# Where the rotation's products are made, and a new order of four engines' work, in a two-layer transformer block

## The reference

```python
x = x + ffn(cond(x, side, lens))
# cond: attention of 16 heads of 16; the keys are x and the query's own key of side, masked by length
score = concat([q @ k_prev.T * SCALE masked, (q * k_self).sum(-1) * SCALE]); attn = softmax(score) ...
# ffn: DEPTH = 2 layers, each on all 4096 rows seen as w windows of 128
h = shift_token(x); q, k, v = split(h @ wqkv, 3)          # 8 heads of 64
q, k = l2norm(q) * qs, l2norm(k) * ksc
q = q * cos * scale + rotate_half(q) * sin * scale        # the rotation
k = k * cos / scale + rotate_half(k) * sin / scale
o = local_attention(q, k, v)                              # own and previous window
x = x + o @ wo
h = layernorm(shift_token(x)); a, g = split(h @ w1 + b1, 2)
x = x + (a * gelu(g)) @ w2 + b2
```

## Time and profile before

| | |
|---|---|
| median of 3 runs | 3763.35 us |
| profiled execution, its own time | 3767.51 us |
| its span | 3765.3 us |
| busy share PE / PE weight load / DVE / ACT / POOL | 96 / 65 / 71 / 60 / 21 % |
| granted TensorE clock, mean | 0.978 |

### The profile page before, as it was taken

The page is one execution under the profiler, slowest core; times in us unless marked ns, Lnnn a source line. Parts: engine busy times, 40 slices in busy tenths (PEclk is TensorE's granted clock), DMA queues, the critical chain, the costliest instruction groups (busy, mean ns, idle before and its releaser), DMA issues.

```text
span 3765.3 us, 58543 instructions
## 1 busy us (share of the span) xinstructions
PE 3602.7 (96%) x20454; PEld 2447.4 (65%) x20454; DVE 2670.4 (71%) x7188; ACT 2242.3 (60%) x5085; POOL 788.4 (21%) x882
## 2 busy tenths in 40 slices
PE   5789999999999999999999999999999999999987
PEld 2456666666666666666666666666666666666655
DVE  2567777777777777777777777777777777777654
ACT  1246566566566666656656656666665665666653
POOL 1122221222222122222122222212222222222110
PEclk7799999999999999999999999999999999999998
DMA  5111110111111011111101111101111110111000
GB/s 144 23 24 23 29 29 20 16 24 29 29 29 29 14 20 26 29 29 29 23 13 24 30 29 29 29 17 19 24 29 29 29 26 13 21 29 24 7 6 9
DMA packets 104608, 99.34 MB, mean 26 GB/s; under 512 B 15276, under 2 KB 103040, under 8 KB 104320
## 3 DMA queue, kind: packets, MB, share of 16 engines
q1 hardware_dynamic: 104320, 95.61, 13.8%
HBM read 35.80 MB, written 8.39 MB: 12 GB/s over the span
## 4 chain that ended last, share of the span: by engine, by line
PE 85%; DVE 7%; issue 3%; ACT 3%; SPq 1%; POOL 0%; DMA 0%; DVEq 0%; ACTq 0%; POOLq 0%
PE ps L994 15%; PE ps L894 12%; PE ps L1007 9%; PE ps L908 6%; PE ps L941 5%; PE ps L961 5%; PE ps L950 4%; PE ps L809 3%; PE ps L970 3%; PE ps L928 3%; PE ps L752 3%; PE ps L762 3%; PE ps L799 3%; PE ps L781 2%; PE ps L834 2%
## 5 line engine op out<-in xcount | busy, mean ns | idle before, releaser
L559 POOL TENSOR_TENSOR inv<-ssq_f,minus_half 128x16 f32<-128x16 f32 x128 | 419.8, 3279 | 1043.9 <-DVE ssq_f L1209 1040.4
L994 PE MATMUL ps<-feed_area,w_s 128*128 128x256 f32 x2560 | 600.7, 382 | 7.3 <-DVE feed_area L1273 6.3
L994 PEld LDWEIGHTS ps<-feed_area,w_s 128*128 128x128 f32 x2560 | 480.5, 191 | 123.2 <-issue 54.1
L657 ACT ACTIVATE attn_area<-attn_area,f_nb,inv 128x128 f32<-128x128 f32 (+1 forms) x1024 | 546.3, 536 | 13.2 <-DVE f_nb L1237 11.6
L1146 DVE TENSOR_REDUCE c_mx<-ps 128x2 f32<-128x512 f32 x512 | 343.2, 687 | 180.5 <-PE ps L781 179.7
L679 ACT ACTIVATE feed_area<-ps,b_s 128x256 f32<-128x256 f32 x320 | 151.0, 473 | 386.3 <-PE ps L994 384.8
L1007 PE MATMUL ps<-feed_area,w_s 128*128 128x256 f32 x1536 | 355.2, 381 | 5.2 <-DVE feed_area L1283 1.5
L610 ACT ACTIVATE cond_area<-ps 128x512 f32<-128x512 f32 x512 | 294.9, 593 | 104.3 <-PE ps L799 103.4
L1233 DVE CUSTOM_DVE_ANT_0 attn_area<-ps,cst 128x128 f32<-128x128 f32 (+1 forms) x1024 | 303.8, 353 | 72.7 <-issue 71.2
L1007 PEld LDWEIGHTS ps<-feed_area,w_s 128*128 128x128 f32 x1536 | 281.7, 190 | 48.9 <-DVE feed_area L1283 14.6
L1283 DVE SCALAR_TENSOR_TENSOR feed_area<-ps,b_s,feed_area 128x256 f32<-128x256 f32 (+1 forms) x384 | 183.8, 479 | 169.0 <-ACT feed_area L679 166.3
(11 more groups left out here) (156 smaller groups left out, 6528.4 us busy)
## 6 DMA issues: line engine op xcount, KB each, us to landing
cond_area<-cond_area SPq DMA_DIRECT2D x384, 128.0 KB, 4.2
x_rows<-in_x SPq DMA_DIRECT2D x32, 256.0 KB, 2.8
f_rows<-in_fside_BxSxS SPq DMA_DIRECT2D x32, 256.0 KB, 3.2
res_rows<-in_x SPq DMA_DIRECT2D x32, 256.0 KB, 2.8
out<-res_rows SPq DMA_DIRECT2D x32, 256.0 KB, 2.1
wqkv_s<-in_L_ffn_wqkv SPq DMA_DIRECT2D x2, 1536.0 KB
w_s<-in_L_ffn_w SPq DMA_DIRECT2D x2, 1364.0 KB
cond_area<-cond_area SPq DMA_DIRECT2D x128, 6.0 KB
```

Of the source, the lines that this page charges most:

```text
L559: nc.gpsimd.tensor_tensor(inv[:, l, t, :], ssq_f[:, l, t, :], minus_half[:, :], ALU.pow).then_inc(SL[l]["inv_norm"], 1)
L657: nc.scalar.activation(soft[:, h % SOFT, lo:hi], soft[:, h % SOFT, lo:hi], ACT.Exp, bias=f_nb[:, l, q, h:h + 1], scale=inv[:, l, q, h:h + ...
L994: last = mm(ps[:, N0 + f % 2, c * N:(c + 1) * N], w1_s[:, l, k, lo:lo + P], hn[:, k, :], start=(k == 0), stop=(k == KD - 1))
```

## The change

Three things change. ACT squares into `ra` instead of `rot[t]`, in a step of its own (`rotate`) and no longer directly behind its second copy; for t = 1 it waits until DVE's sum of t = 0 has read `ra`. POOL makes the two sine products into `rot[t]`, as soon as `qk_s` is there, ahead of the power in its step. DVE keeps the sum of squares, the floor and then the cosine product (into `ra`, over the squares); the final sum of the rotation moves from DVE's step `rotate` to its step `combine`. And all four strings in `ORDER` are new: PE's and DVE's cuts stay, ACT's and POOL's stay in part.

```diff
@@ ORDER
-    PE=((57, 24, 27, 1),
-        "SSARASNASSRRAASRSSAASANRNSSAASNAARARAANAANASANAASANAANSSSSAASAASASAAARSRRANARSRNAASRSASARNASASASRRANA"
+    PE=((57, 24, 27, 1),
+        "NASRARRASRSAASSAARNANASRASSANARASSNAANNSNSAASSANSSSSAAASAASASAAAARAANARASAARRNAARSSAAASRSARAARAASAS"
...
@@ POOL, step rotate
+                    qk4 = qk_s[:, t, :].rearrange("p (s h d) -> p s h d", s=2, h=FH)
+                    pool.wait_ge(SL[l]["qk_copied"], upto(seq, "qk_copied", 2 * t + 2))
+                    for s in range(2):
+                        swapped = qk4[:, s].rearrange("p h (b d) -> p h b d", b=2)[:, :, ::-1, :]
+                        nc.gpsimd.tensor_tensor(
+                            rot[t][:, s * INNER:(s + 1) * INNER].rearrange("p (h b d) -> p h b d", h=FH, b=2),
+                            swapped, sin_t[:, l, t, s].rearrange("p (a b d) -> p a b d", a=1, b=2)
+                            .broadcast_to([P, FH, 2, FDH // 2]), ALU.mult).then_inc(SL[l]["rot_sin"], 1)
@@ ACT
-                    if c == 1:
-                        act.wait_ge(SL[l]["qk_copied"], upto(seq, "qk_copied", 2 * t + 2))
-                        nc.scalar.activation(rot[t], qk_s[:, t, :], ACT.Square).then_inc(SL[l]["squared"], 1)
+                elif name == "rotate":
+                    act.wait_ge(SL[l]["qk_copied"], upto(seq, "qk_copied", 2 * t + 2))
+                    if t == 1:
+
+                        act.wait_ge(SL[l]["rotated"], upto(seq, "rotated", t))
+                    nc.scalar.activation(ra, qk_s[:, t, :], ACT.Square).then_inc(SL[l]["squared"], 1)
@@ DVE, step rotate
-                    dve.wait_ge(SL[l]["qk_copied"], upto(seq, "qk_copied", 2 * t + 2))
-                    if t == 1:
-                        dve.wait_ge(SL[l]["rotated"], upto(seq, "rotated", t))
+                    dve.wait_ge(SL[l]["squared"], upto(seq, "squared", t + 1))
+                    V.tensor_reduce(ssq[:, l, t, :], ra.rearrange("p (h d) -> p h d", d=FDH),
+                                    AX_X, ALU.add).then_inc(SL[l]["sum_squares"], 1)
...
                     V.tensor_tensor(ra.rearrange("p (s h d) -> p s h d", s=2, h=FH), qk4,
                                     cos_t[:, l, t].rearrange("p s (a d) -> p s a d", a=1)
                                     .broadcast_to([P, 2, FH, FDH]), ALU.mult).then_inc(SL[l]["rot_cos"], 1)
-                    dve.wait_ge(SL[l]["squared"], upto(seq, "squared", t + 1))
...
-                    for s in range(2):
...
+                elif name == "combine":
+                    dve.wait_ge(SL[l]["rot_cos"], upto(seq, "rot_cos", t + 1))
                     dve.wait_ge(SL[l]["rot_sin"], upto(seq, "rot_sin", 2 * t + 2))
                     V.tensor_tensor(rot[t], ra, rot[t], ALU.add).then_inc(SL[l]["rotated"], 1)
-                elif name == "combine":
```

30 lines of the change are left out of this document (12 added, 18 removed).

## The result

| | before | after |
|---|---|---|
| median | 3765.51 us (4 runs beside it) | 3938.86 us (4 runs, 3934.53 to 3940.09) |
| ratio | | 1.0456, 95% interval 1.0444 to 1.0469 |
| span of the profiled execution | 3765.3 | 3938.0 |
| a full round, mean of 28 | 111.04 | 116.55 |
| mean granted clock | 0.978 | 0.978 |

The change makes the kernel 4.6% slower: 173 us where 83 were forecast, outside the range. Each of the 29 full rounds is 5.51 us longer, which makes 160 of the 173.

The account below looks back on a forecast made before the run. PE was taken as the bound, 96% busy. Per round 0.29 + 3.29 + 0.80 + 0.48 - 2.0 = 2.86 us, over 29 rounds +83 us, gave 3846 us beside the median of 3763.35; range 3780 to 3915.

Parts of the forecast that it names:

- The sign: Whole kernel: the change was forecast to make it slower, by 83 us; chance of slower 0.83.
- the first two terms: PE, each round: 0.29 us more for crossings to or from part-array steps, and 3.29 us of new waits for banks.
- The edits in themselves: DVE loses 5.6 us a round, POOL gains 10.1, ACT's square moves; none is the bound, each worth nothing by itself.
- The table of bank pairs: PE steps that take a bank soon after an earlier step wait for its copy: 3.29 us a round in all.
- the bank rule: A PE step taking an earlier step's bank waits 0.20 us + copy + 0.05, less PE's work between them.
- two things weighed: POOL products holding DVE (none counted, 1.0 us a round possible) and one more ACT table switch a round (priced 0).
- the hold: POOL's SBUF product slows DVE beside it: four scalings 1.92 us against 1.01 alone; up to 1.26 per sine product, none counted.
- place 3: From the layer's normalisation on, DVE's queue delays the maximum of score 1, then a feed-forward product: 0.80 us a round.
- Rival 2: GpSimd's products hold DVE: 1.0 us of held instructions and 1.1 of lesser queue terms a round, 3907 us; chance 0.18.
- The 0.48: Place 2: four ACT exponentials stand ahead of the prob after turn_max, delaying the prob behind it 0.48 us a round.
- The price of the table switches: ACT, nine switches a round for eight: priced 0 because ACT waits for PE there, at most 37 us.
- The waits of the kernel before: PE's old waits, between 1.0 and 2.74 us a round, taken as 2.0 and subtracted from the new ones.

Follow-up runs that it names:

- e3: Changed kernel with POOL's sine products an eighth as wide, the rest left out: 3885.41 us.
- e7: Changed kernel with POOL's own-key product and low part of the queries cut to an eighth of their columns: 3897.75 us.
- e12: Changed kernel with POOL's sine products, own-key product and low part of the queries all cut to an eighth: 3842.69 us.
- e9: Changed kernel with the square root of layer 1's variance replaced by a plain copy, removing two table loads a round: 3932.22 us.
- e5: Changed kernel with PE's order alone altered at four places to draw bank pairs apart: 3963.63 us.
- e11: Changed kernel without layer 1's square root, and with PE's prob6 moved behind scores01 and qk101 behind prob7: 3933.90 us.
- e13: Changed kernel with ACT's second layer-0 value-row copy ahead of the conditioning value's copy, and PE's prob6 behind scores01: 3906.18 us.
- e14: Kernel before with four steps moved on PE and ACT around the first two probability turns: 3764.43 us against 3764.31.
- e8: Kernel before with two down-projection parts moved later in PE's order, each into a place where PE pauses: 3874.43 us.
- e1: Changed code with the order table of the kernel before, except one moved ACT step: 3912.69 us.
- e2: Code of the kernel before with the new order table: 4094.63 us.

## Why the prediction was wrong

**The sign and the first two terms held.** The edits in themselves came as worked out: POOL's sine products 1280 ns for 1263, DVE relieved of 256 products, no engine a new bound. The table of bank pairs is the best part, measured in the trace after (forecast in brackets): `score` 10 0.32 (0.36), `prob` 2 0.33 (0.39), `prob` 6 0.44 (0.42), second scores 0.18 (0.29), second `qk` 0.63 (0.62), last `turn_max` 0.54 (0.53), `prob` 11 0.44 (0.20), `weigh` 3 0.36 (0.21), and an output projection of each layer 0.24 and 0.19 (0.27 together): 3.66 for 3.29. The pause before layer 1's second projection on X_ffn, whose absence was to refute the bank rule, is there.

**The step that failed** is the first of "two things weighed": "I count none, since most of DVE's instructions then read PSUM, and at most one or two fall on a late place". The row that priced the hold was shown, 1.01 us against 1.92, and was set to 0 in the sum. It was 1.51 us a round for the sine products (e3, 53 us with the partial rounds) and 1.25 for the products of place 3 (e7, 41 us). The error has two parts. POOL's new products were looked at and DVE's three largest instructions on SBUF (L1222, L1226, L1251), which they meet, were not followed through the new order. And POOL's old products, the own-key product and the low part, were not looked at, though the order moves them as well: behind the first rotation's power, which is where DVE now scales keys and tiles. Rival 2 had the mechanism, with 0.18 and 3907 us, and its range, 3880 to 3940, just holds the result; its 1.0 us of held instructions was too small for lack of those two. That the two together took 3.03 us a round (e12) is the size of the term that stood at 0.

**Place 3** was the right place with the wrong reason. 0.80 us were forecast for a long DVE queue. After shows 2.05 (`score` 0 0.86, `score` 2 0.73, `score` 3 0.29, `hidden` 4 0.17), and e12, with the same queue and no hold, 0.10: the queue by itself costs next to nothing. (In e12 the shortened products also hand over their results sooner, but DVE did not wait for them in after either, as its waits above show.)

**The 0.48** for `prob` 10 did not come: PE's pause stands one step on, before `prob` 11, and is in the 0.44 above. The price of the table switches, 0, held: with 2.4 us of loads a round taken away in e9 the round stayed at 116.54.

**The unforecast 1.0** at the end of the round, `turn_probs` 2 (0.44) and in the down projection (0.59), is the hold again: both are 0.01 or less in e3.

**Without the hold the sum stands.** e12 has everything of the change but the hold: 3842.7 us, 78 above the kernel before, and 113.52 us a round, where the forecast had 3846, 83 and 113.9. So the total for the order came out near, and the one effect left at 0 was larger than all the rest together, 96 us against 78. That agreement has some luck in it: 0.48 and 0.80 were forecast and not found, 0.37 more in the pairs while a few waits that had been left out (0.1 to 0.3 each) stand on the other side. The waits of the kernel before, taken off as 2.0, are 2.79 by the comparison of starts.

**What stays open.** Why PE's pauses in e5 and e11 add up to the same is explained for one pair (e13) and only argued for the others. Which of e13's two moves gives its 0.69 us was not run apart. That the removal of a pause before a bank's second use gives back its length was shown in no run by itself. The part up to the end of the third round, which took from 299 to 319 us over the profiles at a mean clock of 0.80 to 0.83, is not explained; between the profiles it differs by up to 20 us, and e14's profile, 11 us short, has rounds of the old length.

## What to carry to other kernels

Before moving an elementwise product to GpSimd, list the VectorE instructions on SBUF that will stand beside it and beside everything of GpSimd's that the new order shifts, and add a full hold for each that somebody waits for; a free engine's work is not free if it stops a bounding queue. When a pause on the bounding engine is to be filled, look first at what the step that fills it hides where it stands, and at whether the copy that is waited for stands behind an instruction that isn't ready: reordering the waiting engine alone moved pauses about or made new ones (e5, e8, e11). Reordering it together with the engine that was waited for removed two pauses once (e13) and gained nothing the other time (e14). Look at the granted clock behind a long pause too: in e1, e2 and e8, with one of 1.9 us or more in each round, about every second round also had 3.4 us at half the clock and was 1.6 to 1.7 us longer.

## What the runs showed of the hardware

- The hold is of whole instructions, as far as the rows of place 3 show, and depends on the form. There L1226 begins 0.99 us before the low part ends (1733.60) and ends 0.54 after it, with 0.69 as its lone length; then L529, begun 0.58 before L1226 ends, ends 1.13 after it, with 1.26 as its lone length. In the trace after, the two-source product of 128x512 on SBUF (L1226) takes 692 ns with no POOL instruction beside it and 1530 beside L549 and L529 (30 times); a scaling of 128x128 (L1251) 281 alone, 1126 beside a sine product (31 times) and 1090 beside L529 (28 times); a product of 4 columns (L1240) 164 alone and 922 (29 times). Not held were, all beside L561: the additions with one source in PSUM (L1121, 692 for 691), the maximum from PSUM (L1157, 679 for 687), the reduction of 128x256 on SBUF (L1148, 609 for 599, with only 4 alone; L1121 has 1) and the reciprocal (L1274, 1743 for 1744). I had not expected that an instruction of 4 columns could lose 0.76 us.
- It goes both ways. POOL's power of 16 columns took 3279 ns before and 3812 in every kernel with the new code and the new order, e12 too (in e1 3.8 us 97 times and 2.9 us 31 times). It is released while DVE runs the sine product (0.69) in the one and the cosine product (1.22) in the other, and 3812 - 3279 is their difference, 0.53, from which I infer that it waits for either to end. The low part (L549) took 1.15 and takes 2.19 above, as it begins 0.05 after DVE's 1.22 us sum.
- The Trainium skill ("GPSIMD Engine Reference", section "Key points") names instructions in a 2-port mode or with two SBUF inputs as those that contend. The held product of two tiles (L1226) and the free sum with a PSUM source (L1121) agree with it. The scaling by a number for each partition has one tile as input and is held, so by that rule it would have to be in a 2-port mode; the trace names no mode, it shows that the scaling takes 64 ns for 128 more columns (345 for 281) where the masking of scores from PSUM (L1236) takes 134 (419 for 285).
- Two table loads a round, 2.4 us of ScalarE, hid completely in its waits for PE: 116.54 us a round with and without them (e9).
- The granted clock fell to half for 3.4 us behind pauses of PE of 1.87 us and more, in 45 of the 84 rounds that had one (e1, e2, e8), and in none of the full rounds of the other kernels, whose longest pause was 1.11 us.
